# Moving two small GpSimd steps ahead of others in a decoder layer on one core

## What is computed

```
x = x + attn(layernorm(x))          # 32 query heads, 8 key/value groups, head size 64, rope, alibi,
                                    # scores capped by 30*tanh(s/30), causal, softmax, then @ Wo + bo
x = x + ssm(ctx, layernorm(x))      # long convolution over 32 heads of k*v products, times q
x = x + ffn(layernorm(x))           # ternary weights, silu(gate)*up, rms norm, projection
layernorm(x) = (x - mean) / sqrt(var + 1e-5)
```

## Time and profile before

| what | value |
|---|---|
| median of 3 runs | 1192.41 us (1191.99 to 1194.55) |
| the profiled execution, its own time | 1191.32 us |
| its span, first to last instruction | 1189.5 us |
| TensorE busy | 1151.5 us, 97% |
| VectorE busy | 875.2 us, 74% |
| GpSimd busy | 698.7 us, 59% |
| ScalarE busy | 534.7 us, 45% |
| mean granted TensorE clock | 0.994 |

### The profile page before, as it was taken

How to read it: one execution, slowest core, us unless ns; L and a number is a source line. 1 busy time by engine, 2 the same in 40 slices (tenths; PEclk the granted TensorE clock), 3 DMA queues, 4 the chain that set the end, 5 groups by cost and what they waited for, 6 DMA issues and landing times. The chain is left out here.

```text
span 1189.5 us, 24884 instructions
## 1 busy us (share of the span) xinstructions
PE 1151.5 (97%) x9763; PEld 798.2 (67%) x9778; DVE 875.2 (74%) x1286; ACT 534.7 (45%) x598; POOL 698.7 (59%) x565
## 2 busy tenths in 40 slices
PE   4879999999999999999999999999999999999998
PEld 3547556757656566576565677777886786786683
DVE  6777988787887787878887788889654744654654
ACT  6666665563755655647556400000342432432341
POOL 0475495784865947849659599998342422322331
PEclk9889999999999999999999999999999999999999
DMA  9445334554445345543455367872001011001000
GB/s 321 138 152 180 120 96 142 154 185 116 133 152 172 117 125 163 187 120 120 128 172 156 145 130 151 144 146 59 1 1 36 6 32 36 18 18 36 19 19 36
DMA packets 153471, 130.34 MB, mean 110 GB/s; under 512 B 56956, under 2 KB 114690, under 8 KB 153410
## 3 DMA queue, kind: packets, MB, share of 16 engines
q1 hardware_dynamic: 128456, 123.29, 35.1%
q10 hardware_dynamic: 24960, 6.29, 3.6%
HBM read 81.76 MB, written 35.21 MB: 98 GB/s over the span
## 5 line engine op out<-in xcount | busy, mean ns | idle before, releaser
L675 PE MATMUL bank<-hT_halves,w_hi 128*128 128x256 f16 x640 | 175.4, 274 | 6.2 <-DVE hT_halves L1376 4.8
L1921 POOL TENSOR_TENSOR parts<-parts 128x512 f32<-128x512 f32 x80 | 119.0, 1490 | 105.1 <-DVE parts L1392 104.0
L676 PE MATMUL bank<-hT_halves,w_hi 128*128 128x256 f16 x640 | 175.0, 273 | 0.0
L677 PE MATMUL bank<-hT_halves,w_lo 128*128 128x256 f16 x640 | 175.0, 273 | 0.0
L923 PE MATMUL bank<-kv,toep 128*128 128x288 f32 (+2 forms) x660 | 157.8, 402 | 0.6 <-ACT qT L1171 0.5
L1926 POOL TENSOR_SCALAR_AFFINE_SELECT region_c<-region_c 128x512 f32<-128x512 f32 x128 | 116.9, 937 | 55.0 <-ACT region_c L1137 55.0
L923 PEld LDWEIGHTS bank<-kv,toep 128*128 128x128 f32 x660 | 123.7, 190 | 34.0 <-ACT qT L1171 0.7
L2069 POOL TENSOR_TENSOR sqsum<-sqsum,toep 128x512 f32<-128x512 f32 x56 | 76.2, 1361 | 102.0 <-ACT toep L1300 101.8
L1134 ACT ACTIVATE region_c<-bank,cap_scale 128x1536 f32<-128x1536 f32 x64 | 98.7, 1542 | 70.6 <-PE bank L743 70.0
L1939 POOL TENSOR_TENSOR ctx_lo<-ctx,ctx_hi 128x512 f16<-128x512 f32 x64 | 95.7, 1496 | 58.8 <-ACT ctx_hi L1113 58.8
L1001 PE MATMUL bank<-odd_halves,guT 128*128 128x256 f16 x512 | 112.4, 273 | 0.0
(11 more groups left out here) (183 smaller groups left out, 2657.8 us busy)
## 6 DMA issues: line engine op xcount, KB each, us to landing
unit_halves<-halves SPq DMA_DIRECT2D x80, 256.0 KB, 2.2
q_both<-unit_halves SPq DMA_DIRECT2D x64, 256.0 KB, 2.9
q_high<-unit_halves SPq DMA_DIRECT2D x64, 128.0 KB, 3.0
toep<-kernel_padded SPq DMA_DIRECT2D x32, 256.0 KB, 3.9
wffn<-w_gu SPq DMA_DIRECT2D x6, 1280.0 KB, 6.2
cpair<-ctx_pairs SPq DMA_DIRECT2D x32, 176.0 KB, 4.7
xin<-x SPq DMA_DIRECT2D x8, 512.0 KB, 3.8
region_o<-wq SPq DMA_DIRECT2D x4, 1024.0 KB, 11.2
```

Of the source, the lines that this page charges most:

```text
L675: pe.matmul(dst, lh, rh, start=first and k == 0, stop=False)
L676: pe.matmul(dst, lh, rl, start=False, stop=False)
L677: mm = pe.matmul(dst, ll, rh, start=False, stop=last and k == n - 1)
L1921: pool.tensor_tensor(slot[:, 0], slot[:, 0], slot[:, 1], ALU.add).then_inc(unit_summed, 1)
```

## The change

It moves instructions on GpSimd alone; the lists of the four other engines stay as they are. There are three edits. In the loop batches, step 7, `keep_x2` and `deviation` go ahead of `add_keys(6)`. In the last batch the block with the 14 deviations goes from step 6 to step 5. At the end of the last batch, the two `products` go behind the last `low_ctx`.

```diff
@@ attend
                 for step in range(STEPS):
                     if step >= 4:
                         low_ctx(b, step - 4)
+                    if step == 7:
+                        keep_x2(b - 1, 4 * TT * b + 2 * TT)
+                        deviation(b + 1, 4 * TT * b + 4 * TT)
                     if 1 <= step < NG + 1:
                         add_keys(b, step - 1)
                     if 2 <= step < 2 + LATE:
                         add_parts(b, EARLY + step - 2)
-                    if step == 7:
-                        keep_x2(b - 1, 4 * TT * b + 2 * TT)
-                        deviation(b + 1, 4 * TT * b + 4 * TT)
                     if step < NG:
                         mask(b, step)
@@ last_batch
-                    if step == 6:
+                    if step == 5:
                         keep_x2(b - 1, 4 * TT * b + 2 * TT)
                         pool.wait_ge(unit_filled, UNITS * B)
                         pool.wait_ge(x2_mv_done, B - 1)
...
                 for g in range(STEPS - 4, NG):
                     low_ctx(b, g)
-                    pool.wait_ge(toep_in[g + 4 - STEPS], 32)
-                    products(g + 4 - STEPS)
+                for n in range(NG + 4 - STEPS):
+                    pool.wait_ge(toep_in[n], 32)
+                    products(n)
```

## The result

The changed kernel takes 1194.97 us (median of 20 runs, 1191.38 to 1198.65) against 1191.57 us (20 runs, 1187.62 to 1194.55) for the kernel before. The ratio is 1.0028 with a 95% interval from 1.0019 to 1.0037, which is 2.3 to 4.4 us slower. The forecast was 1194.9 us and +2.44 us. The profiled execution took 1195.55 us, its span is 1193.8 us.

The account below looks back on a forecast made before the run. The prediction took TensorE, working 97% of the span, as the bound. Its terms for the three edits, 0 + 2.44 + 0 us, on the median of 1192.41 us gave 1194.9 us (+0.20%), range 1192.3 to 1196.8 us.

Parts of the forecast that it names:

- Edit 1 at nothing: Loop batches, step 7: deviation at most 0.3 us sooner, VectorE already has 1.65 us of slack; gain 0.
- margin at mask(7): Loop batches: key sum ends 0.2 us to none before mask(7) can start; loss allowed up to 0.1 us a batch.
- Edit 2, the chain: Last batch: low_ctx(2) and output(2) 3.32 us later, the 0.88 us wait ahead of output(3) goes; net +2.44 us.
- Rival A: Last batch: the 14-column power is not held up beside VectorE's operation; +0.65 us, 1193.1 us, chance 0.18.
- Edit 3 at nothing: End of last batch: products moved behind the last low_ctx still have 4.2 us of cover before TensorE wants them; 0.
- B: Last batch: one further stall reaching TensorE, +4.2 us, 1196.6; or the loop's margin fails, +0.6 more, 1195.5; chance 0.15.
- C: Last batch: unseen slack takes up the delay ahead of output(2); within 0.3 us of 1192.4 us, chance 0.08.
- D: Faster: the loop's 1.4 us of waits and the 0.88 us go, no loss at output(2); 1190.1 us, -0.19%, chance 0.04.

Follow-up runs that it names:

- e7: The changed kernel with 17 further matmuls on TensorE ahead of output(2), filling its wait: 1193.06 us, ratio 1.0019 to the kernel before.
- e3: The changed kernel with VectorE's long 16-bit operation of step 5 of the last batch one step later: 1192.04 us, ratio 1.0004 to the kernel before.
- e1: The kernel before with only the 14 deviations moved from step 6 to step 5 of the last batch: 1195.11 us, ratio 1.0026.
- cut 6 and 8: Kernel before with the 14-column power cut in two, the 8 later: ratios 0.9976 and 0.9998 with edits 1 and 3, 1.0000 without.
- e4: The changed kernel with the 14-column power cut in two, 7 in step 5 and 7 in step 6: 1193.01 us, ratio 1.0015 to the kernel before.
- e2: The kernel before with edits 1 and 3 alone, the 14 deviations staying in step 6: 1191.42 us, ratio 0.9994.
- e10: The kernel before with only the 14-column power cut in 6 and 8, without edits 1 and 3: 1190.69 us, ratio 1.0000.

## Why the prediction was right, and where it was not

**Edit 1 at nothing: right.** The waits for the transposed rows are 1.4 us again, the deviation had 1.76 us of slack instead of 1.65, so it came 0.11 us sooner, and edits 1 and 3 together gave 0.9994 (0.9980 to 1.0008). The margin at mask(7) held, with nothing to spare in the batch shown: the key sum ends at 256.52 + 1.27 = 257.79 and the select starts at 257.82.

**Edit 2, the chain: right, step by step.** The power stood still beside the 16-bit operation: 4.42 us, forecast about 4.4. The wait was 3.79 us, forecast about 3.8. The wait ahead of output(3) went. low_ctx(2) ended 9.68 us after the start of output(1) instead of 6.34, which is 3.34 later; the forecast was 3.32. With the clock kept up the net was +2.38 us, forecast +2.44 (e7). That it was VectorE's operation which held up the power is shown by e3, where moving that operation gave 2.62 us. Rival A, the narrow power passing unhindered, is out. The Trainium skill, page "SBUF — State Buffer", section "SBUF: two separate sides", calls the port pair that VectorE and GpSimd share an exclusive lock, which the one that starts first holds for its whole instruction. This case's trace agrees, now with a narrow instruction as well (4.42 against 2.62 us).

**The sum: one term is missing.** "TensorE starts output(2) 3.32 us later. ... Net: 3.32 - 0.88 = +2.44 us" takes a wait of TensorE at its own length. The profiles showed that TensorE's clock falls to the lower level for some microseconds in or just behind a wait of 2.0 to 3.8 us ahead of output(2). It does so in all five profiles of kernels that had such a wait, and at that place in none of the six with at most 0.9 us of waiting, nor in the one where the wait was filled. This cost 1.4 to 2.9 us more. That the wait brings it on is shown by e7, which fills the wait with matmuls and changes nothing else. The Trainium skill, page "TensorE: Matmul & The Clock Gate", section "HAM oscillation — how this bites in real kernels", describes a matmul kernel whose TensorE stands about 3 to 5 us for a DMA between groups of matmuls and starts each next group at the low clock; the prediction had not weighed it. This case's traces agree that the clock falls, but here single waits of 2.00 and 2.69 us were followed by a fall too, and in e1 and e3 the first matmuls behind the wait still ran at the higher level. By these profiles the changed kernel's stage is 3.8 to 5.3 us longer, +4.6 us as a mean of two. The runs say +2.3 to +4.4 us. The forecast of 2.44 lies inside that interval, near its lower end, so it met the measured difference (+3.4 us) only roughly. That the absolute figure of 1194.9 us was met so closely is luck: the kernel before had run 0.8 us slower in the three runs shown than in the 20, and this made up for most of the missing 1 us. The chain was right; the term for the clock was put at nothing, without a reason.

**Edit 3 at nothing: right.** The products stand where they were expected, products(0) from 673.68 and products(1) until 678.76, ahead of the convolution at 680.69:

```profile
672.56 1.17 POOL L1939 TENSOR_TENSOR ctx_lo<-ctx,ctx_hi 128x512 f16<-128x512 f32 x1 [5.08 <-ACT ctx_hi L1113]
673.68 2.16 POOL L1971 TENSOR_TENSOR kv<-cpair 128x1024 f32<-128x1024 f32 x1
675.81 0.65 POOL L1972 TENSOR_TENSOR kv<-cpair 128x128 f32<-128x128 f32 x1
676.42 1.91 POOL L1971 TENSOR_TENSOR kv<-cpair 128x1024 f32<-128x1024 f32 x1
678.29 0.47 POOL L1972 TENSOR_TENSOR kv<-cpair 128x128 f32<-128x128 f32 x1
```

**The rivals.** B's further stall did not come: no second TensorE wait appeared in the stage. C and D did not come either. The wait ahead of output(3) that D wanted to save is saved without a loss in the cut 6 and 8, where the block stays behind low_ctx(2) and only its first part stands ahead of low_ctx(3).

**What stays open.** How long the clock stays down differs between executions of the same kernel (2.9 and 1.4 us lost), and nothing here says by what it is set. Whether the fall comes in every execution of the changed kernel is not known: three profiles of edit 2 in that form show it, and the mean clocks of edit 2 alone fit it. In the kernels where the clock fell, the stage's excess lies about 1 us or more above what the runs give: 4.6 against 3.4 us in the changed kernel, 4.05 against 3.1 (e1), 2.9 against 1.8 (e4), 2.3 against 0.5 (e3). In e7, where it held, the two agree (2.38 and 2.3). So the clock may cost less in most executions than in those profiled; this was not looked into.

## What to carry to other kernels

Move a result ahead only if its reader waits for it. Here VectorE was held by a DMA and by its own order, and in edit 2 the block that GpSimd was made to do first delayed a low context for which TensorE already waited. Edits 1 and 3 held up nothing that an engine waited for, and cost nothing. Before placing work on GpSimd, look at what VectorE runs at that moment. And when an engine that is otherwise always busy comes to stand for some microseconds, count the clock that it may lose, not only the wait.

## What the hardware showed that I had not expected

A TensorE wait of only 2.00 us (e3) was followed by matmuls 0.43 us apart, with 1.6 us lost on top of the wait; in the stage, waits of up to 0.9 us cost nothing more. In e3 the first three matmuls behind the wait still ran at the higher level:

```profile
648.02 0.39 PE L675 MATMUL bank<-region_o,ctx_hi 128*128 128x512 f16 x1 [2.00 <-POOL ctx_lo L1939]
648.25 0.38 PE L676 MATMUL bank<-region_o,ctx_hi 128*128 128x512 f16 x1
...
649.01 0.63 PE L676 MATMUL bank<-region_o,ctx_hi 128*128 128x512 f16 x1
649.43 0.63 PE L677 MATMUL bank<-region_o,ctx_lo 128*128 128x512 f16 x1
```

A long wait is not the only place where the clock falls. Near the end of the convolution TensorE stands 0.42 to 0.43 us in every profile, and there the clock fell in three of the twelve profiles, one of them of the changed kernel and two of kernels without a long wait (e2 and e10). In the other nine it stayed up at the same place, behind the same wait. So at this place the length of the wait does not tell whether the clock falls; it cost 1.1 to 1.4 us more. Here e10:

```profile
831.59 0.66 PE L959 MATMUL bank<-ident_s,hbuf 128*128 128x128 f32 x4 [0.43 <-DVE prod L1758]
...
834.00:838.00 4.00, 4.00 (x16) 3.40 (x16) 2.37 (x5) 0.16 (x1) 2.71 (x3) 0.70 0.00 0
```

In the profiles, seventeen useless matmuls in a wait were cheaper than standing still: the stage got shorter by 1.4 to 2.9 us. The run times do not confirm that gain.
